# Attention stage: the score-times-value batches moved to the odd slots, with the two transposes placed directly ahead of a batch

## The chip, the core and the metric

The kernel runs on one core of a Trainium2 chip. The metric is the device time of one execution in microseconds (us). Five engines work beside each other, each through its own instruction stream in order: PE (TensorE: matrix products and transposes into PSUM banks; its weight loads are listed as PEld), DVE (VectorE), ACT (ScalarE), POOL (GpSimd) and SP (SyncE, which here only issues DMAs). They meet through semaphores: an instruction waits until a counter has reached a value.

## What is computed (the reference, cut)

```python
# x: (32 sequences, 4 channels, 250 positions); model width 64
h = tok(x, ...)                                    # 8 steps of a two-way recurrence
h = h + attn(layernorm(h), ...)                    # 8 heads of width 64
h = h + ffn(layernorm(h), ...)                     # 16 experts, the best 2 for each token

# attn, for each head:
xn = layernorm(x) * ln_scale
Q, K, V = xn @ W_q, xn @ W_k, xn @ W_v
sqdist = max(|q|^2 + |k|^2 - 2 q.k, 0)
scores = exp(-gamma * sqdist)                      # no division by a row sum
out = concat over heads of (scores @ V) @ W_o.T
```

The change touches the attention stage alone.

## The kernel before, in words

The program has three stages: the recurrence, the attention, and the mixture of experts. The 32 sequences are handled as 16 pairs, and each engine's stream is written out by hand; the order in the source is the order on the engine.

The attention stage is a software pipeline of 18 steps. In step p the engines make the projections of pair p (`new`), the scores of pair p-1 (`old`), and finish pair p-2 (`old2`). A step has eight slots, v = 0 to 7. These are the pieces, with the short names used below:

- **Token transposes** (`tokens_b`, L1064): four PE transposes that turn the normalised tokens `xn` of a pair into columns in bank 0. ACT (`round_b`, L523 and L527) and DVE (`stack_b`, L763) then make the operand `s1` of them.
- **Units u0 to u15** (`unit`, L1131 and L1135): two matmuls each, into banks 2, 3, 4 in turn. So unit k waits until unit k-3 has been read out. u0 to u7 are squared by ACT (L560), summed by POOL (L411) and DVE (L799). The four units u8, u10, u12, u14 (L1135) are read twice, first by ACT (L555, two instructions), then by DVE (L805, two instructions); u9, u11, u13, u15 are copied by ACT (L564). Slot 0 has no unit, slots 1 and 2 have three each, slots 3 to 7 two each.
- **Score products** (`scores`, L1107 and L1109): two matmuls for each of two chunks in a slot, in banks 5 to 7. ACT takes the exponential (L546), DVE clips it (`caps`, L790) in a buffer `prob`, of which there are four.
- **A batch**: the products `prob` x `u` (L1083) of two slots, 16 small matmuls in column halves, accumulated in bank 1. There are four batches for each pair. After the second and the fourth ACT copies bank 1 out (`evac_y`, L538).
- **Fold** (`fold_b`, L1091): four transposes of a finished pair into bank 0; DVE adds them to the residual (L780, L783).
- **The query and key norms**: when the eighth L799 reduction of a step is done (it stands behind u8's L805 and one clip on DVE), POOL makes `qkw` (L415, L418); PE transposes it in slot 5 (L1166), ACT and DVE make the operand `s2` of it (L584, L830), and SP carries two of its rows elsewhere by DMA.
- **The next pair's normalisation** on POOL: behind `qkw` in the same stream, ten instructions from L381 to L400, each waiting for the one before; the last, L400, writes `xn`, which the next token transposes wait for (`b_xn`).

On PE a step of the kernel before reads: token transposes; slot 0: scores, batch; slot 1: scores, u0 to u2, fold; slot 2: scores, u3 to u5, batch; slot 3: scores, u6, u7; slot 4: scores, u8, u9, batch; slot 5: scores, u10, u11, transposes of `qkw`; slot 6: scores, u12, u13, batch; slot 7: scores, u14, u15.

Of the kernel before, what the change touches and what calls it, by code (L numbers as in the profile page):

```python
# [72 lines left out]
def build(nc, cst, xin, xparts, aw1, aw2, cw1, cw2, w24, wqT, wkT, wvT, woT, wq, wk, gam, lns,  # L73
          gw, gb, w1, b1, w2, b2, fg, fb, out):
    with ExitStack() as ctx:
# [100 lines left out]
        b_xt, b_rnd, b_s1 = sem("b_xt"), sem("b_rnd"), sem("b_s1")  # L176
# [36 lines left out]
        def first_step(p):  # L213
            return p == 0
# [271 lines left out]
        def _(act):  # L486
# [53 lines left out]
            def step_b(p, j, old2, old, new, ln):  # L540
                def exps(v, c):
                    n = 2 * v + c
                    n += 16 * (p - 1)
                    act.wait_ge(b_sc, n + 1)
                    wait(act, b_pv, 8 * (p - 1) + v - 3)
                    act.activation(prob[v % PROBS][:, :, c, :], bank[5 + n % 3][0:T, 0:C].rearrange("p (h l) -> p h l", h=2),  # L546
                                   ACT.Exp).then_inc(b_exp, 1)

                def unit(k):
                    src = bank[2 + k % 3]  # L550
                    act.wait_ge(b_pj, 16 * p + k + 1)
                    if is_g(k):
                        wait(act, b_sc, 16 * (p - 1))
                        for a in range(2):
                            last = act.activation(m1[j][64 * a:64 * a + 64, k - 8 + a, :],  # L555
                                                  src[64 * a:64 * a + 64, 0:C], ACT.Copy)
                        last.then_inc(b_ev, 1)
                    elif k < 8:
                        wait(act, b_sum, 8 * p + k - 1)
                        act.activation(sq[k % 2][:, :, :], src[0:T, :].rearrange("p (h d) -> p h d", h=H), ACT.Square)\  # L560
                            .then_inc(b_ev, 1)
                    else:
                        wait(act, b_pv, 8 * (p - 1))
                        act.activation(u_sb[j][:, (k - 8) // 2, :], src[0:T, :], ACT.Copy).then_inc(b_ev, 1)  # L564

                for v in range(8):
                    if new and v == 0 and not first_step(p):
                        round_b(p, j)
                    rest = list(units(v)) if new else []
                    for c in range(2):  # L570
                        if old:
                            exps(v, c)
                        if rest:
                            unit(rest.pop(0))
                    if v == 0 and old2:
                        evac_y(p - 2, 1)
                    if v == 4 and old:
                        evac_y(p - 1, 0)
                    for k in rest:
                        unit(k)  # L580
                    if new and v == 5:
                        act.wait_ge(b_qt, p + 1)
                        wait(act, b_s2, p)
                        act.activation(rnd2[64:S_ROWS, :], bank[0][64:S_ROWS, 0:C], ACT.Copy).then_inc(b_rnd2, 1)  # L584
                    if p == PAIRS:
                        start_c(v)
# [80 lines left out]
        def _(dve):  # L667
# [117 lines left out]
            def step_b(p, j, old2, old, new, ln):  # L785
# [27 lines left out]
                for v in range(8):  # L813
                    if new and v == 0 and not first_step(p):
                        stack_b(p, j)
                    rest = list(units(v)) if new else []
                    for c in range(2):
                        if old2 and v == 3 and c == 0:
                            residual(p - 2, 1)
                        if rest:  # L820
                            unit(rest.pop(0))
                        if old:
                            caps(v, c)
                    for k in rest:
                        unit(k)
                    if v == 2 and old2:
                        residual(p - 2, 0)
                    if new and v == 5:
                        dve.wait_ge(b_rnd2, p + 1)
                        dve.scalar_tensor_tensor(s2[j][64:S_ROWS, :], f32(rnd2[64:S_ROWS, :]),  # L830
                                                 c_sb[64:S_ROWS, C_MS2:C_MS2 + 1], bank[0][64:S_ROWS, 0:C],
                                                 ALU.mult, ALU.add).then_inc(b_s2, 1)
                    if ln and v == 0:
                        norm_stats(p + 1, b_ln)
                    if ln and v == 1:
                        norm_aggr(p + 1, b_ln)
                    if p == PAIRS:
                        start_c(v)
# [143 lines left out]
        def _(pe):  # L982
# [77 lines left out]
            def tokens_b(p):  # L1060
                pe.wait_ge(b_xn, p + 1)
                wait(pe, b_s2, p)
                for c in range(CH):
                    last = pe.transpose(bank[0][:, c * T:(c + 1) * T],  # L1064
                                        xn[:, c, :, :].rearrange("p a d -> p (a d)"), ident[0:T, 0:T])
                last.then_inc(b_xt, 1)
# [28 lines left out]
            def step_b(p, j, old2, old, new, ln):  # L1095
# [41 lines left out]
                    last.then_inc(b_pj, 1)  # L1137

                for v in range(8):
                    if new and v == 0 and not first_step(p):  # L1140
                        tokens_b(p)
                    if old and v == 0:
                        pe.wait_ge(b_row, 32 * p)
                    rest = list(units(v)) if new else []
                    for c in range(2):
                        if old:
                            scores(v, c)
                        if rest:
                            unit(rest.pop(0))
                    for k in rest:  # L1150
                        unit(k)
                    for n in (v - 2, v - 1) if v % 2 == 0 else ():
                        for hh in range(2):
                            if v == 0 and old2:
                                products(p - 2, n + 8, j, hh)
                            if v > 0 and old:
                                products(p - 1, n, o, hh)
                    if old2 and v == 1:
                        if new:
                            pe.wait_ge(b_s1, p + 1)  # L1160
                        fold_b(p - 2)
                    if new and v == 5:
                        pe.wait_ge(b_qkw, 2 * p + 2)
                        wait(pe, b_res, p - 1)
                        for c in range(CH):
                            last = pe.transpose(bank[0][0:S_ROWS, c * T:(c + 1) * T], qkw[:, c, :], ident[0:T, 0:T])  # L1166
                        last.then_inc(b_qt, 1)
                    if p == PAIRS:
                        start_c(v)
# [191 lines left out]
```

## Time and profile before

| | |
|---|---|
| median of 3 runs | 797.2 us (796.36 to 800.66) |
| the profiled execution | 796.95 us, of which the span from first to last instruction is 795.1 us |
| granted TensorE clock, mean | 0.981 of full speed |
| busy share of the span | PE 95%, DVE 78%, ACT 67%, POOL 59% |
| attention stage, whole steps | from 139.6 us to 462.9 us, 13 steps of 24.87 us |

A step is read from one pair's token transposes to the next pair's. The times in the rows are microseconds from the start of the span.

### The profile page before, as it was taken

Reading aid. Unit: us, or ns where it says so; the run is one execution under the profiler, and the core shown is the slowest. Engines: PE = TensorE matmul, PEld = TensorE weight load, DVE = VectorE, ACT = ScalarE, POOL = GpSimd, SP = SyncE. Lnnn points to the kernel's source line nnn. Section 1 sums busy time; section 2 is a strip of 40 time slices with the busy share of each in tenths; the row PEclk is TensorE's granted clock in tenths of the full one; section 3 lists DMA queues with packets and bytes.
Section 4 is the critical chain, followed back from the end, with each engine's and each line's share of the span. In section 5 each row is a group of like instructions: output and inputs, shape, how many; then the busy total and the mean of one; then the engine's idle time right before and its main releaser. Section 6 shows DMA issues by size and latency. Waiting matters only on the chain.

```text
span 795.1 us, 16732 instructions
## 1 busy us (share of the span) xinstructions
PE 751.7 (95%) x5680; PEld 435.9 (55%) x5680; DVE 620.8 (78%) x1524; ACT 534.4 (67%) x1058; POOL 468.6 (59%) x628
## 2 busy tenths in 40 slices
PE   2999879999999999999999998999999999999992
PEld 1343456666666666766667665535445455454441
DVE  3677657888878888788887886688888888888862
ACT  0566578888888888888888888554554555545442
POOL 8650256455464554645556452257888788887877
PEclk9999969999999999999999999899999999999997
DMA  6400021112211122111221112000000000000000
GB/s 151 137 2 2 1 54 29 40 41 54 54 29 40 42 54 54 28 40 41 55 54 28 40 42 54 1 2 2 9 8 15 9 8 9 9 15 8 8 8 19
DMA packets 22859, 25.69 MB, mean 32 GB/s; under 512 B 12888, under 2 KB 21720, under 8 KB 22648
## 3 DMA queue, kind: packets, MB, share of 16 engines
q1 hardware_dynamic: 21608, 23.57, 12.8%
q10 hardware_dynamic: 1168, 1.07, 0.6%
q8 instruction: 46, 0.75, 0.4%
q14 instruction: 37, 0.30, 0.1%
HBM read 5.30 MB, written 2.43 MB: 10 GB/s over the span
## 4 chain that ended last, share of the span: by engine, by line
PE 72%; DVE 11%; ACT 6%; issue 6%; POOL 3%; DMA 1%; SPq 0%; POOLq 0%; ACTq 0%; DVEq 0%
PE bank L1220 14%; PE bank L1198 13%; PE bank L1083 10%; PE bank L1131 9%; PE bank L1011 6%; PE bank L1107 6%; DVE m L805 5%; PE bank L1109 5%; DVE prob L790 4%; ACT m L555 3%; PE bank L1001 2%; ACT prob L546 1%; PE bank L1245 1%; PE bank L1237 1%; PE bank L1253 1%
## 5 line engine op out<-in xcount | busy, mean ns | idle before, releaser
L790 DVE TENSOR_SCALAR prob<-prob,cap_hi,cap_lo 125x500 f32<-125x500 f32 x256 | 155.8, 636 | 45.5 <-ACT prob L546 43.4
L411 POOL TENSOR_TENSOR sq<-sq 125x256 f32<-125x256 f32 x128 | 97.9, 776 | 151.1 <-ACT sq L560 127.3
L546 ACT ACTIVATE prob<-bank 125x500 f32<-125x500 f32 x256 | 148.9, 592 | 40.8 <-PE bank L1109 38.8
L1198 PE MATMUL bank<-cs,w_sb 64*64 64x500 f32 x1024 | 147.3, 580 | 2.5 <-DVE gated L921 2.4
L1220 PE MATMUL bank<-gated,w_sb 64*64 64x500 f32 x1024 | 149.1, 588 | 0.0
L448 POOL TENSOR_TENSOR gated<-relu,wb 128x500 f32<-128x500 f32 x96 | 120.2, 1253 | 48.3 <-ACT relu L645 45.8
L921 DVE SCALAR_TENSOR_TENSOR gated<-bank,nb,wb 128x500 f32<-128x500 f32 x160 | 114.9, 727 | 34.5 <-PE bank L1198 34.5
L1083 PE MATMUL bank<-prob,u 125*64 125x250 f32 x1024 | 127.4, 386 | 1.9
L645 ACT ACTIVATE relu<-bank,b_sb 128x500 f32<-128x500 f32 x96 | 64.7, 674 | 92.6 <-PE bank L1198 92.6
L1107 PE MATMUL bank<-m,s 128*125 128x500 f32 x256 | 111.5, 435 | 0.2 <-DMA m<-s 0.2
L805 DVE TENSOR_TENSOR m<-bank,m 64x500 fp32r<-64x500 f32 x128 | 86.5, 676 | 27.5 <-ACT m L555 26.2
L1109 PE MATMUL bank<-m,s 112*125 112x500 f32 x256 | 101.2, 395 | 0.0
L1083 PEld LDWEIGHTS bank<-prob,u 125*64 125x64 f32 x1024 | 65.4, 137 | 58.9 <-DVE prob L790 24.7
L1131 PE MATMUL bank<-wqku_hi,s 128*125 128x512 f32 x192 | 79.7, 415 | 5.8 <-DVE s L763 3.0
L1198 PEld LDWEIGHTS bank<-cs,w_sb 64*64 64x64 f32 x1024 | 52.9, 133 | 55.4 <-issue 48.8
L560 ACT ACTIVATE sq<-bank 125x512 f32<-125x512 f32 x128 | 75.6, 600 | 7.7 <-PE bank L1131 3.7
L1131 PE MATMUL bank<-wqku_lo,s 128*125 128x512 f32 x192 | 77.5, 404 | 0.0
L555 ACT ACTIVATE m<-bank 64x500 fp32r<-64x500 f32 x128 | 74.0, 578 | 1.0 <-PE bank L1135 0.2
L1220 PEld LDWEIGHTS bank<-gated,w_sb 64*64 64x64 f32 x1024 | 46.8, 132 | 45.4 <-issue 38.6
L1107 PEld LDWEIGHTS bank<-m,s 128*125 128x125 f32 x256 | 48.3, 189 | 30.4 <-issue 17.8
L1011 PE MATMUL bank<-st_a,w_sb 64*64 64x500 f32 x224 | 58.2, 591 | 0.0
L1011 PE MATMUL bank<-st_b,w_sb 64*64 64x500 f32 x224 | 57.4, 591 | 0.0
(171 smaller groups left out, 1319.1 us busy)
## 6 DMA issues: line engine op xcount, KB each, us to landing
m<-m SPq DMA_DIRECT2D x128, 125.0 KB, 2.3
out<-res SPq DMA_DIRECT2D x16, 125.0 KB
xa<-xparts SPq DMA_DIRECT2D x4, 281.2 KB
w_sb<-in_w SPq DMA_DIRECT2D x1, 1024.0 KB
xw<-xparts SPq DMA_DIRECT2D x4, 140.6 KB
w_sb<-in_w SPq DMA_DIRECT2D x1, 512.0 KB
m<-s SPq DMA_DIRECT2D x32, 15.6 KB
xparts<-x_part SPq DMA_DIRECT2D x1, 375.0 KB, 4.5
```

Of the source, the lines that this page charges most:

```text
L448: gp.tensor_tensor(gated[g % 8][:, :], relu_sb[n % 3][:, :], wb[q % 2][:, :], ALU.mult).then_inc(c_gatep, 1)
L546: act.activation(prob[v % PROBS][:, :, c, :], bank[5 + n % 3][0:T, 0:C].rearrange("p (h l) -> p h l", h=2), ACT.Exp).then_inc(b_exp, 1)
L790: dve.tensor_scalar(part, part, cap_hi[0:T, h:h + 1], cap_lo[0:T, h:h + 1], ALU.min, ALU.max)\
L805: last = dve.tensor_tensor(m2[j][0:64, h, :], bank[2 + k % 3][rows, 0:C], f32(m1[j][rows, h, :]), ALU.subtract)
L921: dve.scalar_tensor_tensor(gated[g % 8][:, :], up_bank(g)[:, 0:C], nb1[:, g:g + 1], wb[q % 2][:, :], ALU.max, ALU.mult).then_inc(c_gated, 1)
L1011: last = pe.matmul(dst[cols, 0:C].rearrange("p (b l) -> p b l", b=2), w24_sb[rows, 0, :], src[rows, :, 0:L], start=False, stop=True)
L1083: last = pe.matmul(bank[1][64 * c:64 * c + 64, 0:L], u_sb[jj][:, 2 * b + c, h * D:(h + 1) * D], prob[v % PROBS][:, hh, c, :], start=h == 0 ...
L1107: pe.matmul(ps, s1[o][:, cols], m1[o][:, 2 * hp:2 * hp + 2, b * L:(b + 1) * L], start=True, stop=False)
L1109: pe.matmul(ps, s2[o][:, cols], m2[o][:, 2 * hp:2 * hp + 2, b * L:(b + 1) * L], start=False, stop=True).then_inc(b_sc, 1)
L1131: last = pe.matmul(dst[0:T, :], s1[j][:, c * T:(c + 1) * T], w[:, q, :], start=first, stop=not first)
L1198: last = pe.matmul(up_bank(g)[cols, 0:C], w1_sb[rows, g, cols], cs1[q % 3][rows, :], start=True, stop=True)
L1220: last = pe.matmul(y[cols, 0:C], w2_sb[rows, g, :], gated[g % 8][rows, :], start=v == 0, stop=v == 7, skip_group_check=True)
```

## The change

On PE the batches move from the even slots to the odd ones, each of them one slot later. The fold moves from slot 1 to slot 3, directly ahead of the batch there, and the explicit wait for `b_s1` ahead of it goes (u0 waits for that semaphore too). The token transposes of the next pair move from the head of the next step to the end of slot 7, behind u15 as now, but ahead of the batch of that slot. On ACT the two `evac_y` move two slots later; on DVE the two residual instructions move two slots later.

```diff
@@ ACT, step_b @@
-                    if v == 0 and old2:
+                    if v == 2 and old2:
                         evac_y(p - 2, 1)
-                    if v == 4 and old:
+                    if v == 6 and old:
                         evac_y(p - 1, 0)
@@ DVE, step_b @@
-                        if old2 and v == 3 and c == 0:
+                        if old2 and v == 5 and c == 0:
                             residual(p - 2, 1)
...
-                    if v == 2 and old2:
+                    if v == 4 and old2:
                         residual(p - 2, 0)
@@ PE, step_b @@
                 for v in range(8):
-                    if new and v == 0 and not first_step(p):
-                        tokens_b(p)
...
-                    for n in (v - 2, v - 1) if v % 2 == 0 else ():
+                    if old2 and v == 3:
+                        fold_b(p - 2)
+                    if ln and v == 7:
+                        tokens_b(p + 1)
+                    for n in (v - 3, v - 2) if v % 2 else ():
                         for hh in range(2):
-                            if v == 0 and old2:
+                            if v == 1 and old2:
                                 products(p - 2, n + 8, j, hh)
-                            if v > 0 and old:
+                            if v > 1 and old:
                                 products(p - 1, n, o, hh)
-                    if old2 and v == 1:
-                        if new:
-                            pe.wait_ge(b_s1, p + 1)
-                        fold_b(p - 2)
```

On PE, around the end of a step: the last unit u15 (into bank 2), the token transposes (into bank 0), and what follows them, in the kernel before. L1107 and L1109 are the score products, L1083 the batch.

```order
L1131 MATMUL bank2<-wqku_hi,s1_0 125x512
L1131 MATMUL bank2<-wqku_lo,s1_0 125x512
L1064 MATMUL bank0<-c_sb,xn 128x125 x4
L1107 MATMUL bank7<-m1_0,s1_0 125x500
L1109 MATMUL bank7<-m2_0,s2_0 125x500
L1107 MATMUL bank5<-m1_0,s1_0 125x500
L1109 MATMUL bank5<-m2_0,s2_0 125x500
L1083 MATMUL bank1<-prob2,u1 64x250 x4
L1083 MATMUL bank1<-prob3,u1 64x250 x4
```

The same place in the changed kernel:

```order
L1131 MATMUL bank2<-wqku_hi,s1_0 125x512
L1131 MATMUL bank2<-wqku_lo,s1_0 125x512
L1064 MATMUL bank0<-c_sb,xn 128x125 x4
L1083 MATMUL bank1<-prob0,u1 64x250 x4
L1083 MATMUL bank1<-prob1,u1 64x250 x4
L1107 MATMUL bank7<-m1_0,s1_0 125x500
L1109 MATMUL bank7<-m2_0,s2_0 125x500
L1107 MATMUL bank5<-m1_0,s1_0 125x500
L1109 MATMUL bank5<-m2_0,s2_0 125x500
```

The batch behind the token transposes is the one (of `prob0` and `prob1`) that stood in slot 6 before, ahead of u14 and u15; the one of `prob2` and `prob3` now follows in slot 1.

On PE, from u9 (into bank 2) to u11 (into bank 4) in slots 4 and 5 of the kernel before; u8, just ahead, went into bank 4 too, and the L1135 rows are u10 (into bank 3).

```order
L1131 MATMUL bank2<-wqku_hi,s1_0 125x512
L1131 MATMUL bank2<-wqku_lo,s1_0 125x512
L1083 MATMUL bank1<-prob2,u1 64x250 x4
L1083 MATMUL bank1<-prob3,u1 64x250 x4
L1107 MATMUL bank7<-m1_1,s1_1 125x500
L1109 MATMUL bank7<-m2_1,s2_1 125x500
L1135 MATMUL bank3<-s1_0,wg_hi 128x500
L1135 MATMUL bank3<-s1_0,wg_lo 128x500
L1107 MATMUL bank5<-m1_1,s1_1 125x500
L1109 MATMUL bank5<-m2_1,s2_1 125x500
L1131 MATMUL bank4<-wqku_hi,s1_0 125x512
L1131 MATMUL bank4<-wqku_lo,s1_0 125x512
```

The same place in the changed kernel:

```order
L1131 MATMUL bank2<-wqku_hi,s1_0 125x512
L1131 MATMUL bank2<-wqku_lo,s1_0 125x512
L1107 MATMUL bank7<-m1_1,s1_1 125x500
L1109 MATMUL bank7<-m2_1,s2_1 125x500
L1135 MATMUL bank3<-s1_0,wg_hi 128x500
L1135 MATMUL bank3<-s1_0,wg_lo 128x500
L1107 MATMUL bank5<-m1_1,s1_1 125x500
L1109 MATMUL bank5<-m2_1,s2_1 125x500
L1131 MATMUL bank4<-wqku_hi,s1_0 125x512
L1131 MATMUL bank4<-wqku_lo,s1_0 125x512
L1083 MATMUL bank1<-prob2,u1 64x250 x4
L1083 MATMUL bank1<-prob3,u1 64x250 x4
```

No batch stands between u8 and u11 any more; it comes behind u11. In the same way the batch between u12 and u15 has gone behind u15.

On DVE, slot 4 and the start of slot 5 in the changed kernel: the read of u8 (L805 from bank 4), the clips, the eighth reduction (L799), and the two residual instructions (L780, L783).

```order
L805 TENSOR_TENSOR m2_1<-bank4,m1_1 64x500 x2
L790 TENSOR_SCALAR prob0<-prob0,cap_hi,cap_lo 125x500
L799 TENSOR_REDUCE qk<-sq2_1 125x8
L790 TENSOR_SCALAR prob0<-prob0,cap_hi,cap_lo 125x500
L780 TENSOR_TENSOR z2<-bank0,h_all 125x256
L783 TENSOR_TENSOR h_all<-bank0,z2 125x256
L805 TENSOR_TENSOR m2_1<-bank3,m1_1 64x500 x2
L790 TENSOR_SCALAR prob1<-prob1,cap_hi,cap_lo 125x500 x2
```

In the kernel before the rows are the same without L780 and L783, which stood in slots 2 and 3: the eighth reduction keeps its place behind u8's L805 and one clip.

## Rows read from the trace of the kernel before

**Rows 1.** The page, part 1: busy time and share of each engine.

```profile
PE 751.7 (95%) x5680; PEld 435.9 (55%) x5680; DVE 620.8 (78%) x1524; ACT 534.4 (67%) x1058; POOL 468.6 (59%) x628
```

**Rows 2.** The waits: who waited for whom, us in total, times, longest.

```profile
PEld bank L1083 <- DVE prob L790: 24.7, 66, 0.6
...
PEld bank L1064 <- POOL xn L400: 6.1, 15, 1.6
```

**Rows 3.** Timeline of PE in one step: start, duration, engine, line, operands.

```profile
263.88 0.65 PE L1064 MATMUL bank<-c_sb,xn 125*128 125x125 f32 x4
...
265.38 2.29 PE L1083 MATMUL bank<-prob,u 125*64 125x250 f32 x16
...
277.10 0.39 PE L1135 MATMUL bank<-s,wg_hi 128*128 128x500 f32 x1
...
278.24 0.39 PE L1131 MATMUL bank<-wqku_lo,s 128*125 128x512 f32 x1
278.56 1.91 PE L1083 MATMUL bank<-prob,u 125*64 125x250 f32 x16
280.40 0.49 PE L1107 MATMUL bank<-m,s 128*125 128x500 f32 x1
280.73 0.39 PE L1109 MATMUL bank<-m,s 112*125 112x500 f32 x1
280.95 0.40 PE L1135 MATMUL bank<-s,wg_hi 128*128 128x500 f32 x1
...
284.25 0.50 PE L1131 MATMUL bank<-wqku_hi,s 128*125 128x512 f32 x1
284.59 0.39 PE L1131 MATMUL bank<-wqku_lo,s 128*125 128x512 f32 x1
...
288.74 0.65 PE L1064 MATMUL bank<-c_sb,xn 125*128 125x125 f32 x4
```

**Rows 4.** Timeline of PE: token transposes of the third and of the last pair.

```profile
139.57 0.65 PE L1064 MATMUL bank<-c_sb,xn 125*128 125x125 f32 x4
...
462.88 0.65 PE L1064 MATMUL bank<-c_sb,xn 125*128 125x125 f32 x4
```

**Rows 5.** Timeline of DVE in the same step as Rows 3.

```profile
274.70 0.41 DVE L780 TENSOR_TENSOR z<-bank,h_all 125x256 f32<-125x256 f32 x1
...
280.91 0.41 DVE L799 TENSOR_REDUCE qk<-sq 125x8 f32<-125x256 f32 x1
...
284.23 0.99 DVE L790 TENSOR_SCALAR prob<-prob,cap_hi,cap_lo 125x500 f32<-125x500 f32 x2
...
287.61 1.80 DVE L790 TENSOR_SCALAR prob<-prob,cap_hi,cap_lo 125x500 f32<-125x500 f32 x2
```

**Rows 6.** Timeline of POOL in the same step; in brackets the idle time before.

```profile
281.40 0.55 POOL L415 TENSOR_TENSOR qkw<-qk,gneg 125x64 f32<-125x64 f32 x1 [2.41 <-DVE qk L799]
...
282.47 1.02 POOL L383 TENSOR_TENSOR inv<-inv,mhalf 125x4 f32<-125x4 f32 x1
...
284.41 1.23 POOL L391 TENSOR_TENSOR inv<-inv,mhalf 125x4 f32<-125x4 f32 x1
...
287.39 1.29 POOL L400 TENSOR_TENSOR xn<-z,lns_sb 125x512 f32<-125x512 f32 x1
```

**Rows 7.** Timeline of PE where the attention stage ends.

```profile
489.88 2.12 PE L1083 MATMUL bank<-prob,u 125*64 125x250 f32 x16
494.10 0.62 PE L1237 MATMUL bank<-c_sb,cxn 125*128 125x125 f32 x4 [2.10 <-ACT cxn L613]
```

**Rows 8.** Windows of PE: stretch, length, busy (instructions), granted clock, DMA share, GB/s.

```profile
493.00:494.00 1.00, 0.00 (x0) 1.00 0.00 0
...
496.00:497.00 1.00, 1.00 (x15) 0.50 0.00 0
...
501.00:502.00 1.00, 1.00 (x8) 0.50 0.00 0
```

**Rows 9.** Groups by line: count, busy us, mean ns, idle us before.

```profile
L538 ACT ACTIVATE y_att<-bank 128x250 f32<-128x250 f32 x32 | 12.2, 382 | 15.6 <-PE bank L1083 15.6
```

## The prediction

> **What bounds the kernel now.** The page's first part comes first: PE is busy 95% of the span, the other engines 78% and less [rows 1]. By that alone PE is the bound, and every wait taken from PE is time won. The list of waits says which there are: PE's weight loads stood 24.7 us before clips (66 times, about one for each of the 64 batches), and 6.1 us, 15 times, before POOL's `xn` [rows 2]. The first sum looks like the prize. The timeline of PE in one step corrects that: a batch in slot 4 begins 0.32 us after the last matmul of a unit (278.24 to 278.56) and takes 1.91 us, the one in slot 0 takes 2.29 us [rows 3]. So of the time before clips only 0.38 us for each step is lost on PE, in slot 0; the rest is a fixed step into the batch's other shape.
>
> The second sum is the smaller one, and it is the one that matters. The last of POOL's ten instructions ends at 287.39 + 1.29 = 288.68 [rows 6], and PE's token transposes begin at 288.74 [rows 3], 0.06 us later. They don't begin when PE has come to them; they begin when `xn` is there. It is a wait that hardly shows, because PE comes there at about the same moment. Followed back: POOL's stretch begins at 281.40 with L415, which stood idle 2.41 us until DVE's L799 [rows 6]; that reduction ends at 280.91 + 0.41 = 281.32 [rows 5], 4.22 us after u8 began on PE at 277.10 [rows 3]. So there are two paths from u8 to the next token transposes, each of 11.64 us (277.10 to 288.74): PE's own work, and the path u8 - ACT - DVE - L799 (4.22) - POOL (288.68 - 281.32 = 7.36) - `xn`. From the transposes on to the next u8 there is PE's own work alone: 277.10 - 263.88 = 13.22 [rows 3]. Together 24.86, and the 13 whole steps (462.88 - 139.57)/13 give 24.87 [rows 4].
>
> **The change part by part.** The sum is made for a step, as time from token transposes to u8, and from u8 to token transposes.
>
> *What a batch costs PE.* From the last unit matmul before it to the second score matmul behind it 280.73 - 278.24 = 2.49 us; without the batch two matmul starts of 0.23 each (five of them from 277.10 to 278.24 make 1.14). So 2.03.
>
> *From the transposes to u8.* Now two batches lie there (slots 0 and 2). In the changed order there are three: one directly behind the transposes, one in slot 1, one in slot 3 behind the fold. That adds 2.03. The clip wait of slot 0 goes: -0.38. The step into a batch partly coincides with the transposes, and u8 now stands behind a batch, so that ACT and DVE are free for it: I take 0.15 off for both, an estimate between 0 and 0.3. The sum is 13.22 + 2.03 - 0.38 - 0.15 = 14.7.
>
> *From u8 to the transposes, on PE.* Two batches become one: 11.64 - 2.03 = 9.6. But a batch has covered something there. u13 waits for the bank of u10 (u10 at 280.95, u13 at 284.25, its second matmul 0.34 later) [rows 3]: 3.30 us is what ACT and DVE need for such a unit, and PE now loses about 0.11 before u13 and 0.11 behind, 0.22. In the changed order this pair is covered by a batch (-0.22), while u8 to u11 and u12 to u15 stand without one: six pairs of matmuls of 0.46 are 2.75, so PE waits 3.30 - 2.75 = 0.55, and 0.11 behind, twice: +1.3. PE would be there after 9.6 - 0.2 + 1.3 = 10.7.
>
> *From u8 to the transposes, by POOL.* Nothing in that path is shortened. The eighth reduction stands on DVE behind u8's L805 and one clip, as before (the residual instructions come behind it), and POOL's ten follow. 11.6 us remain. PE, there after 10.7, waits some 0.9, and the batch in slot 7 that could be done meanwhile stands behind the waiting transposes in PE's stream. Everything else on PE waits with it; ACT and DVE have caught up by then, and wait for PE.
>
> So a step is 14.7 + 11.6 = 26.3 to 26.4 instead of 24.87: +1.5. Bounds: 1.3 (0.3 off, as above) and 1.65 (nothing off), and the same whatever u11 and u15 lose, as long as that stays under the 0.9.
>
> *POOL's stretch beside other work.* Its instructions are longer beside clips: L391 took 1.23 where its like L383 took 1.02 [rows 6], while two clips that take 0.99 together took 1.80 beside L400 [rows 5]. In the changed order other clips fall beside POOL's last three. I take nothing for it and keep +-0.2 a step. The Trainium skill has a harder rule (SBUF — State Buffer, Who interferes with whom): of a VectorE and a GpSimd instruction that need the shared port pair, the later one is blocked until the first has ended. If a clip came just ahead of L400, that would add up to one clip, half of 0.99, to each step, +6 us in all; L400 at 1.29 beside the clips of 1.80 agrees with the rule, with POOL first.
>
> *Parts that I cost at nothing.* `evac_y` (0.38 each [rows 9]) in slot 6 must be done before the batch of slot 7 may write bank 1: that batch now waits for `xn` anyway, over 1 us longer than ACT needs. The residual pair on DVE (0.41 each [rows 5]) lies ahead of u10's L805, whose bank u13 needs only after a batch; uncovered it would cost 0.8. The removed wait for `b_s1` is made by u0. The `qkw` transposes come behind the batch of slot 5, and ACT waits at L584 for them with the exponentials of slot 6 queued behind; PE has three score banks and the unit banks ahead, so it doesn't run dry; if it did, u15 would be later, inside the 0.9. SP's DMAs keep their order and are issued earlier relative to their use.
>
> *First and last steps.* Up to the third pair's transposes (139.57) nothing is lost: step 1 has the same batches on both sides. Then 13 steps x 1.5 = 19.5. After the last token transposes the changed order has one batch more to do than now (2.03), without the losses of slot 0 and u13 (-0.38 - 0.22), with those of u11 and u15 (2 x 0.66): +2.7. The first transposes of the expert stage stand idle 2.10 for ACT's normalisation [rows 7]; that wait stays, since in the changed order the exponentials stand ahead of it as now.
>
> Sum: 796.95 (the profiled execution: 795.1 of span and 1.85 around it) + 19.5 + 2.7 = 819.2; the median of the runs shown, 797.2, is 0.25 above the profiled one. I predict 819.
>
> **Rivals.**
>
> *POOL's path gives way.* If `xn` came earlier than I think, PE would set the step: 14.7 + 10.7 = 25.4, +0.55 x 13 + 2.7 = +10, 807. Against it: all ten instructions and what they wait for are unchanged.
>
> *PE alone counts (faster).* PE's share of 95% speaks for it. Then only losses are removed, 0.38 in slot 0, 0.22 at u13, and some 0.05 at the transposes: -0.65 x 14 = -9, 788. It decides if L400 ends over 1.5 us earlier relative to u8 and u11 doesn't wait; against it the 0.06 us in rows 3 and 6, and the 3.30 between u10 and u13.
>
> *The waits only change places (same).* If the won 0.6 and the lost 1.3 met with a POOL path that is shorter by just that, the step would stay at 24.9: 797 to 800.
>
> *The clock falls.* In the changed order PE would stand idle three times in each step, about 0.5, 0.5 and 0.7 us. After an idle of 2.10 [rows 7] the granted clock fell from 1.00 (2.4 GHz) to 0.50 (1.2 GHz), and six windows in a row, 496 to 502, read 0.50 [rows 8]. If each step lost as much, six such microseconds at half speed would cost 3 a step, 13 x 3 = 39 more: 858. Against it: the idle times are shorter by far and not in one piece. The Trainium skill speaks for it (TensorE: Matmul & The Clock Gate, A second HAM failure mode: psum-queue depth-cycling): frequent short idles between groups of matmuls, as banks are cycled, can make the clock swing between its levels. By that rule the time would be this rival's 858; no row here shows it for idles under 1 us.
>
> **How the numbers follow.** The forecast: 0.78, by itself 814 to 825. POOL's path gives way: 0.07. PE alone: 0.06. Waits change places: 0.04. Clock: 0.05. The range of 8 in 10 takes in the forecast and the first rival, 806 to 826, with POOL's +-0.2 a step (2.6). A measurement can tell 0.5% (4 us) from no change: faster 0.06, same 0.04, slower 0.90.
>
> **What would show it.** Right: token transposes 26.2 to 26.5 apart, beginning 0.05 to 0.06 after L400's end, PE idle ahead of them, L400 still 7.4 after the eighth reduction; u11 and u15 waiting for L805, u13 not; batches all of 1.91, none with 2.29. Wrong: steps of 25.4 or less, or transposes that begin well after `xn` is there, or windows of the steady steps with a clock of 0.50, or waits of POOL that are shorter from the reduction to `xn`.

## The result and the profile after

The changed kernel takes 830.0 us (median of 4 runs, 826.9 to 837.3); the kernel before, run beside it, 797.4. The ratio is 1.0415, with a 95% interval of 1.0341 to 1.0489: slower. The prediction said 819 with a range of 806 to 826. The direction and the mechanism held, the size didn't, and the time lies outside the range.

The profiled execution of the changed kernel took 826.9 us, with a span of 825.1. The page's first part answers to [rows 1]; the columns are the same.

```profile
PE 755.5 (92%) x5680; PEld 443.3 (54%) x5680; DVE 618.4 (75%) x1524; ACT 526.8 (64%) x1058; POOL 472.8 (57%) x628
```

Every engine does the same number of instructions as before, and TensorE is busy 3.8 us longer in a span that is 30.0 us longer. So 26 of the 30 us are idle time of TensorE. The list of waits answers to [rows 2].

```profile
PEld bank L1131 <- DVE m L805: 31.1, 32, 2.3
PEld bank L1064 <- POOL xn L400: 21.3, 15, 2.0
...
PE bank L1064 <- POOL xn L400: 14.8, 15, 1.6
...
PEld bank L1083 <- DVE prob L790: 7.5, 22, 0.5
```

The waits for clips, which looked like the prize, fell from 24.7 to 7.5 us. The wait for `xn`, which looked small, is now in TensorE's own list: 14.8 us, 15 times. And the value units u11 and u15 wait for L805, 32 times.

The timeline of TensorE in one step answers to [rows 3].

```profile
193.97 0.65 PE L1064 MATMUL bank<-c_sb,xn 125*128 125x125 f32 x4 [0.98 <-POOL xn L400]
194.54 1.91 PE L1083 MATMUL bank<-prob,u 125*64 125x250 f32 x16
...
208.90 0.39 PE L1135 MATMUL bank<-s,wg_hi 128*128 128x500 f32 x1
...
212.19 0.50 PE L1131 MATMUL bank<-wqku_hi,s 128*125 128x512 f32 x1 [0.40 <-DVE m L805]
...
216.55 0.40 PE L1131 MATMUL bank<-wqku_hi,s 128*125 128x512 f32 x1
...
219.08 0.50 PE L1131 MATMUL bank<-wqku_hi,s 128*125 128x512 f32 x1 [0.54 <-DVE m L805]
219.41 0.39 PE L1131 MATMUL bank<-wqku_lo,s 128*125 128x512 f32 x1
220.78 0.65 PE L1064 MATMUL bank<-c_sb,xn 125*128 125x125 f32 x4 [0.97 <-POOL xn L400]
```

From token transposes to u8 it is 208.90 - 193.97 = 14.93, from u8 to the next token transposes 220.78 - 208.90 = 11.88, together 26.81 where before it was 24.86. u11 and u15 wait, u13 (216.55) doesn't; the batch takes 1.91; TensorE stands idle 0.97 before the transposes. GpSimd's and VectorE's timelines of the same step answer to [rows 5, 6].

```profile
213.12 0.55 POOL L415 TENSOR_TENSOR qkw<-qk,gneg 125x64 f32<-125x64 f32 x1 [4.00 <-DVE qk L799]
...
215.85 0.46 POOL L389 TENSOR_TENSOR inv<-inv,eps 125x4 f32<-125x4 f32 x1
216.39 1.18 POOL L391 TENSOR_TENSOR inv<-inv,mhalf 125x4 f32<-125x4 f32 x1
...
219.31 1.41 POOL L400 TENSOR_TENSOR xn<-z,lns_sb 125x512 f32<-125x512 f32 x1
```

```profile
212.63 0.41 DVE L799 TENSOR_REDUCE qk<-sq 125x8 f32<-125x256 f32 x1
...
219.06 1.94 DVE L790 TENSOR_SCALAR prob<-prob,cap_hi,cap_lo 125x500 f32<-125x500 f32 x2
```

L400 ends at 219.31 + 1.41 = 220.72, 0.06 before the transposes: GpSimd's path binds, in each of the 13 whole steps. The reduction ends at 213.04, 4.14 after u8 began (before 4.22). From there to the end of L400 it is 7.68 us, where before it was 7.36. Two instructions make the difference: L400 takes 1.41 for 1.29 [rows 6], and L389 takes 0.46 (L391 is 0.05 shorter); the kernel before has

```profile
284.13 0.20 POOL L389 TENSOR_TENSOR inv<-inv,eps 125x4 f32<-125x4 f32 x1
```

Three of the 13 steps are longer still, 28.4 us. In these TensorE's clock fell, which it did in no whole step of the kernel before. First TensorE's timeline, then its windows of one microsecond (stretch, length, busy, granted clock, DMA share, GB/s), which answer to [rows 8].

```profile
246.19 0.40 PE L1131 MATMUL bank<-wqku_lo,s 128*125 128x512 f32 x1
247.56 0.99 PE L1064 MATMUL bank<-c_sb,xn 125*128 125x125 f32 x4 [0.97 <-POOL xn L400]
248.47 3.19 PE L1083 MATMUL bank<-prob,u 125*64 125x250 f32 x16
```

```profile
247.00:248.00 1.00, 0.44 (x3) 0.86 0.93 202
248.00:249.00 1.00, 1.00 (x7) 0.50 0.68 150
...
250.00:251.00 1.00, 1.00 (x6) 0.50 0.00 0
```

The batch behind the transposes took 3.19 instead of 1.91 us, and such a step lost 1.63 us. The same happens at 357 and 466 us. Now the account closes: 13 steps of +1.92 make 25.0, three falls of 1.63 make 4.9, the steps up to the third pair's transposes cost 0.7 (they begin at 140.26, before at 139.57), and after the last transposes the changed kernel needs 331.5 us, 0.7 less than before. 25.0 + 4.9 + 0.7 - 0.7 = 29.9, and the spans differ by 30.0.

### The profile page after: what moved, and what is told of

It is laid out like the page before. It is cut to its first block, busy times and chain, and to the rows that moved or that the text cites. A ratio compares the mean times of both kernels' runs of the same rounds, so it can differ in the third digit from the quotient of the medians.

```text
span 825.1 us, 16718 instructions
## 1 busy us (share of the span) xinstructions
PE 755.5 (92%) x5680; PEld 443.3 (54%) x5680; DVE 618.4 (75%) x1524; ACT 526.8 (64%) x1058; POOL 472.8 (57%) x628
## 4 chain that ended last, share of the span: by engine, by line
PE 71%; POOL 13%; DVE 7%; ACT 3%; issue 3%; ACTq 1%; DMA 1%; POOLq 0%; DVEq 0%
PE bank L1218 14%; PE bank L1196 13%; PE bank L1083 12%; PE bank L1131 7%; PE bank L1011 6%; PE bank L1107 5%; PE bank L1109 4%; DVE m L805 3%; POOL xn L400 2%; ACT m L555 2%; POOL inv L391 2%; POOL inv L383 2%; PE bank L1001 2%; PE bank L1064 1%; DVE prob L790 1%
## 5 line engine op out<-in xcount | busy, mean ns | idle before, releaser
L790 DVE TENSOR_SCALAR prob<-prob,cap_hi,cap_lo 125x500 f32<-125x500 f32 x256 | 152.2, 622 | 65.5 <-ACT prob L546 63.4
L1083 PE MATMUL bank<-prob,u 125*64 125x250 f32 x1024 | 126.4, 390 | 0.1
L805 DVE TENSOR_TENSOR m<-bank,m 64x500 fp32r<-64x500 f32 x128 | 86.3, 674 | 34.5 <-ACT m L555 33.1
L1107 PE MATMUL bank<-m,s 128*125 128x500 f32 x256 | 107.6, 420 | 0.0
L1109 PE MATMUL bank<-m,s 112*125 112x500 f32 x256 | 101.1, 395 | 0.0
L1131 PE MATMUL bank<-wqku_hi,s 128*125 128x512 f32 x192 | 81.4, 424 | 20.4 <-DVE m L805 17.5
L1083 PEld LDWEIGHTS bank<-prob,u 125*64 125x64 f32 x1024 | 69.8, 140 | 44.6 <-issue 10.7
L1107 PEld LDWEIGHTS bank<-m,s 128*125 128x125 f32 x256 | 48.2, 188 | 27.2 <-issue 17.9
L1131 PEld LDWEIGHTS bank<-wqku_hi,s 128*125 128x125 f32 x192 | 36.7, 191 | 42.8 <-DVE m L805 31.1
```

Source lines behind the costliest of these rows:

```text
L790: dve.tensor_scalar(part, part, cap_hi[0:T, h:h + 1], cap_lo[0:T, h:h + 1], ALU.min, ALU.max)\
L805: last = dve.tensor_tensor(m2[j][0:64, h, :], bank[2 + k % 3][rows, 0:C], f32(m1[j][rows, h, :]), ALU.subtract)
L1083: last = pe.matmul(bank[1][64 * c:64 * c + 64, 0:L], u_sb[jj][:, 2 * b + c, h * D:(h + 1) * D], prob[v % PROBS][:, hh, c, :], start=h == 0 ...
L1107: pe.matmul(ps, s1[o][:, cols], m1[o][:, 2 * hp:2 * hp + 2, b * L:(b + 1) * L], start=True, stop=False)
L1109: pe.matmul(ps, s2[o][:, cols], m2[o][:, 2 * hp:2 * hp + 2, b * L:(b + 1) * L], start=False, stop=True).then_inc(b_sc, 1)
L1131: last = pe.matmul(dst[0:T, :], s1[j][:, c * T:(c + 1) * T], w[:, q, :], start=first, stop=not first)
```

## The experiments

Ten kernels were run. "Step" is the time from one pair's token transposes to the next pair's. The table gives the median time of the runs, and from each trace the usual step among those where the clock did not fall, its two parts, and by how much the transposes begin after `xn` is ready. The row of e6 comes from an execution whose clock was lower throughout (see there).

| kernel | us | step | to u8 | from u8 | after `xn` |
|---|---|---|---|---|---|
| before | 797.4 | 24.87 | 13.22 | 11.64 | 0.05 |
| changed | 830.0 | 26.79, three 28.4 | 14.91 | 11.88 | 0.05 |
| e1 transposes behind the batch | 818.9 | 26.52 | 13.83 | 12.69 | 0.84 |
| e2 scales early | 811.7 | 26.05 | 14.83 | 11.22 | 3.52 |
| e3 batch (4,5) alone | 832.2 | 26.53, five 28.13 | 14.90 | 11.63 | 0.06 |
| e4 filler | 824.0 | 26.82 | 14.91 | 11.91 | 0.06 |
| e5 short clips | 807.6 | 25.72 | 14.89 | 10.83 | 0.06 |
| e6 batch (6,7) alone | 832.4 | 26.87, four 28.4 | 15.0 | 11.88 | 0.61 |
| e7 the same, scales early | 825.1 | 26.65 | 14.85 | 11.81 | 3.65 |
| e8 before, scales early | 807.8 | 25.62 | 13.01 | 12.61 | 3.55 |
| e9 before, scales spread | 795.2 | 24.79 | 13.18 | 11.60 | 3.83 |
| e10 the same, `xn` held | 794.1 | 24.62 | 13.02 | 11.60 | 1.25 |

**e1: the token transposes behind the batch of slot 7.** Of the changed kernel, so that TensorE doesn't stand with a batch queued behind its wait.

```diff
-                    if ln and v == 7:
-                        tokens_b(p + 1)
                     for n in (v - 3, v - 2) if v % 2 else ():
                         ...
+                    if ln and v == 7:
+                        tokens_b(p + 1)
```

> The changed kernel with one part undone: the token transposes stand behind the batch of slot 7 again, just ahead of the next step's scores. Theory (PE stands idle before the transposes because xn comes 11.9 us after u8, and the batch of slot 7 is queued behind them): that batch now fills the wait, so u8 to transposes is set by PE, 10.8 + 2.0 = 12.8, with no idle of a microsecond ahead of the transposes and no window of the steady steps at a clock of 0.50. Behind the transposes the cover for u0 is gone: u0 waits some 0.7 us for s1, so transposes to u8 is 14.9 - 2.05 + 0.7 = 13.6. Step 26.3 to 26.4, time 797 + 13 x 1.5 = 816. Rival (the loss is that u8 to u11 and u12 to u15 stand without a batch; where the transposes stand is no matter): as the changed kernel, 827 to 830, step 26.8.

Measured: 818.9 us, ratio 1.0261 (1.0232 to 1.0290). The step is 26.52, 0.1 above what was expected, no whole step shows a clock below 1.00, and the wait for `xn` is gone. In its place TensorE waits for the next pair's operand `s1`:

```profile
272.49 0.65 PE L1064 MATMUL bank<-c_sb,xn 125*128 125x125 f32 x4
...
275.26 0.46 PE L1131 MATMUL bank<-wqku_hi,s 128*125 128x512 f32 x1 [0.73 <-DVE s L763]
```

The batch in slot 7 had covered the way from the transposes through ScalarE and VectorE to u0, and without it u0 waits.

**e2: GpSimd's seven scale instructions ahead of its wait for the eighth reduction.** Of the changed kernel. They don't need that reduction, and only stood behind it in GpSimd's stream.

```diff
+                    if ln:
+                        b_scales(p + 1)          # L381 to L393 of before
                     gp.wait_ge(b_red, 8 * p + 8)
                     ...
                 if ln:
-                    b_scales(p + 1)
+                    b_tokens(p + 1)              # the last three, to xn
```

> The changed kernel, PE, ACT and DVE untouched; on POOL the seven small instructions of the next pair's normalisation (L381 to L393) stand ahead of the wait for the eighth reduction, where POOL is idle for 3.95 us. Theory: xn is there 3 to 4 us earlier relative to u8, the wait before the transposes goes, PE sets the stretch from u8 to the transposes at 10.8 and the step at 14.9 + 10.8 = 25.7; no clock of 0.50 in the steady steps; time 797 + 13 x 0.85 = 808, the rest of the loss being the two waits of u11 and u15 (0.65 and 0.75). Rival (POOL's path is not what PE waits for, the batches' missing cover is): 827 to 830, step 26.8.

Measured: 811.7 us, ratio 1.017 (1.0141 to 1.0199); the step is 26.05, 0.35 more than expected. GpSimd's path is out of the way and 18 us of the 33 came back: by the two profiled executions 15.3, of which the 13 shorter steps make 9.6 and the clock falls that did not come 4.9. TensorE's own order keeps the rest: behind u8 it is 11.22 instead of 11.64, though a batch of 2.03 has left that side, since u11 waits 0.40 and u15 0.95 there. The 0.35 stand at u15 (lines are 5 higher than before in this kernel): TensorE's timeline and VectorE's.

```profile
293.39 0.50 PE L1136 MATMUL bank<-wqku_hi,s 128*125 128x512 f32 x1 [0.95 <-DVE m L810]
293.73 0.39 PE L1136 MATMUL bank<-wqku_lo,s 128*125 128x512 f32 x1
293.96 0.59 PE L1069 MATMUL bank<-c_sb,xn 125*128 125x125 f32 x4
```

```profile
289.56 1.61 DVE L795 TENSOR_SCALAR prob<-prob,cap_hi,cap_lo 125x500 f32<-125x500 f32 x2
291.20 0.74 DVE L835 SCALAR_TENSOR_TENSOR s<-rnd,c_sb,bank 48x500 fp32r<-48x500 f32 x1
291.97 1.36 DVE L810 TENSOR_TENSOR m<-bank,m 64x500 fp32r<-64x500 f32 x2
```

The last GpSimd instruction (1.30 us from 289.14 on) now runs beside two clips, which take 1.61 instead of 0.99; the rounding residual behind them comes 0.6 later, measured from u8, the L805 behind that 0.5 later, and u15 waits 0.95 instead of 0.54.

**e3: one batch alone.** The kernel before, with only the batch (4,5) moved from slot 6 to behind the next token transposes in slot 7.

```diff
-                    for n in (v - 2, v - 1) if v % 2 == 0 else ():
+                    if ln and v == 7:
+                        tokens_b(p + 1)
+                    for n in {0: (-2, -1), 2: (0, 1), 4: (2, 3), 7: (4, 5)}.get(v, ()):
```

> The kernel before with one part of the change alone: only the batch of slot 6 moves, to the end of slot 7 behind the token transposes; the other three batches, the fold, evac_y and the residual stay in their old slots, and u8 to u11 keeps its batch. Theory (two paths of 11.6 to 11.9 from u8 to the transposes; work taken from PE's path ahead of them only makes PE wait, and it has to be done behind them): the step grows by the whole batch, 14.85 + 11.7 = 26.5, less or more 0.2; 797 + 13 x 1.7 = 819, up to 824 if the clock falls in some steps. Rival (the loss is the missing cover of u11 and u15): only u15 loses 0.75 and slot 0 wins its 0.38, 24.87 + 0.4 = 25.3, 802.

Measured: 832.2 us, ratio 1.0414 (1.0368 to 1.0461). The step is the theory's, and the time lies above it by the clock: it fell in five of the 13 steps (1.6 each) and twice more behind the last transposes, from where this kernel needs 4.8 us more than the one before. One batch of four, moved past the token transposes, makes 1.66 of the changed kernel's 1.92 a step: from u8 to the transposes it is still 11.63, since GpSimd sets that, and the other part has the batch on top. TensorE now idles where the batch had been:

```profile
273.25 0.50 PE L1131 MATMUL bank<-wqku_hi,s 128*125 128x512 f32 x1 [1.30 <-DVE m L805]
274.33 0.95 PE L1064 MATMUL bank<-c_sb,xn 125*128 125x125 f32 x4 [0.35 <-POOL xn L400]
```

**e4: the idle time filled.** The changed kernel with four matmuls, read by nobody, in the wait for `xn`.

```diff
+                    if ln and old and v == 7:
+                        wait(pe, b_s2, p + 1)
+                        for _ in range(FILL):                # FILL = 4
+                            pe.matmul(bank[0][0:T, :], s1[j][:, 0:T], wqku_hi[:, 0, :], start=True, stop=True)
                     if ln and v == 7:
                         tokens_b(p + 1)
```

> The changed kernel with four matmuls that nobody reads (0.23 us each) on PE between u15 and the token transposes of every step, in the time when PE waits for xn. Theory (POOL sets the step, and three of the 13 steps are 1.6 us longer because the clock falls after the idle ahead of the transposes): the step stays at 26.8, L1064 still begins 0.05 after L400 ends, and no window of the steady steps reads a clock of 0.50; 827 - 3 x 1.6 = 822, and the executions agree with each other. Rival 1 (the clock falls for another reason): 827 to 830, with windows of 0.50. Rival 2 (PE is the bound): the step grows by 0.9, 827 + 12 = 839.

Measured: 824.0 us, ratio 1.0323 (1.029 to 1.0356). More work on TensorE, and a faster kernel: its four runs (822.4 to 825.4) lie below all four of the changed one. All 13 steps take 26.80 to 26.84, and in none of them does the clock fall below 1.00; the end of one wait:

```profile
301.11 0.40 PE L1131 MATMUL bank<-wqku_lo,s 128*125 128x512 f32 x1
301.34 1.08 PE L1155 MATMUL bank<-wqku_hi,s 128*125 128x512 f32 x4
302.49 0.65 PE L1064 MATMUL bank<-c_sb,xn 125*128 125x125 f32 x4
```

So in the changed kernel the falls hang on the idle time ahead of the transposes, and they are a loss of their own on top of it. Without them the changed order takes 824.0 us.

**e5: short clips.** The changed kernel, in which the clips work on 16 columns instead of 500 (most of the clipping is left out).

```diff
-                    part = prob[v % PROBS][:, hh, :, :]
+                    part = prob[v % PROBS][:, hh, :, 0:8]
```

> The changed kernel with VectorE's clips cut from 500 to 16 columns (most of the clipping is left out; VectorE's instruction count and every wait stay). Theory: GpSimd's ten instructions from the eighth reduction to the normalized tokens take 7.69 us in the changed kernel because VectorE's clips run beside them (the last one, 1.42 us, beside a clip that takes 1.49 instead of 0.54); the same chain without clips beside it, at the second pair, took 6.88. So the chain falls to 6.9 to 7.1 and the last instruction to 1.27 to 1.30; reductions and residuals come earlier too, and the step falls from 26.79 to 25.4 to 26.1, about 808 to 815 us. Rival: the added 0.31 us of the chain comes from something else than the clips (the residual of the rounded scales, ScalarE, or the place in the step): the chain stays at 7.5 or above and the step above 26.4, at 818 us or more.

Measured: 807.6 us (one run), step 25.72. GpSimd's stretch from the eighth reduction to `xn` takes 6.88 us instead of 7.68, at every step. Three of its instructions:

```profile
288.45 0.20 POOL L389 TENSOR_TENSOR inv<-inv,eps 125x4 f32<-125x4 f32 x1
288.73 1.01 POOL L391 TENSOR_TENSOR inv<-inv,mhalf 125x4 f32<-125x4 f32 x1
...
291.49 1.27 POOL L400 TENSOR_TENSOR xn<-z,lns_sb 125x512 f32<-125x512 f32 x1
```

0.20, 1.01 and 1.27 where the changed kernel has 0.46, 1.18 and 1.41, and the one before 0.20, 1.23 and 1.29. So it is VectorE's clips that lengthen GpSimd's path, by 0.8 us in the changed kernel and by 0.5 in the one before.

**e6: the batch (6,7) alone, to slot 1.** Since e3 had shown that batches are needed in slots 4 and 6, this one left them there and moved the one that waited 0.38 us for clips in slot 0.

```diff
-                    for n in (v - 2, v - 1) if v % 2 == 0 else ():
+                    for n in {1: (-2, -1), 2: (0, 1), 4: (2, 3), 6: (4, 5)}.get(v, ()):
```

> The kernel before with only the batch of products (6,7) moved, from slot 0 to slot 1; fold, evacuation and residuals follow it as in the change (slots 3, 2, 4 and 5); the batches of slots 2, 4 and 6 and the token transposes stay. Theory: batches at slots 4 and 6 are what covers the waits for the value units' banks, and they stay; the batch that waited 0.38 us for clipped probabilities at slot 0 no longer does, so the step falls from 24.87 to about 24.49 and the time to 792 (790 to 794.5). Rival: any batch that is taken out of slot 0 leaves the path through GpSimd as long as it was and the residuals in slots 4 and 5 lengthen it (VectorE's queue): step 24.9 to 25.3, 798 to 803 us.

Measured: 832.4 us, ratio 1.0451 (1.0413 to 1.0488). My theory fell, and the rival that I had set beside it was not the cause either: the transposes begin 0.61 us after `xn`, so GpSimd's path does not bind. The mean clock of five of its runs was 0.97, which is part of it, but the step itself shows the main thing:

```profile
279.45 0.60 PE L1064 MATMUL bank<-c_sb,xn 125*128 125x125 f32 x4
...
283.25 0.47 PE L1131 MATMUL bank<-wqku_hi,s 128*125 128x512 f32 x1 [1.81 <-DVE s L763]
```

The batch in slot 0 covered a wait as well, that of u0 for `s1`. It paid 0.38 us for clips, and hid 1.8. I had e1's row with the same wait before me, and didn't draw on it. The profiled execution was the longest of the six (840.9 us, mean clock 0.927), and its windows read 0.95 where those of the other kernels read 1.00:

```profile
277.00:278.00 1.00, 1.00 (x8) 0.95 0.06 10
```

So its figures are not to be compared to the hundredth. e7, at 1.00, has the same wait.

**e7 and e8: the scales early, in e6 and in the kernel before.** The edit is that of e2.

> The same with GpSimd's scale instructions ahead of its wait for the eighth reduction, so that the token transposes never wait for GpSimd. Theory: TensorE bounds the step in it and in the kernel before as well (transposes 0.27 us after the matmul ahead of them), so the early scales take away 0.05 us a step at most: 24.44 to 24.5, 791 to 792 us. Rival: the path through GpSimd bounds the step there too, and its release gives 0.3 us a step or more: 24.2 or below, 788 us or less. Second rival: the last GpSimd instruction now falls beside a clip ahead of VectorE's rounding residual and delays the last value unit, as in the run with early scales of the changed kernel (0.46 us a step): 24.9, 797 us.

> The kernel before with GpSimd's scale instructions ahead of its wait for the eighth reduction and nothing else. Theory: no change, since TensorE bounds the step of the kernel before and the path through GpSimd ends just ahead of it: step 24.8 to 24.87, 796 to 798 us. Rival: the delayed clip costs 0.3 to 0.5 us a step, 801 to 804 us.

Measured: e7 825.1 us, ratio 1.0338 (1.031 to 1.0367); e8 807.8, ratio 1.0118 (1.0092 to 1.0145). e7 rests on e6's mistake: u0 still waits, here with the clock at 1.00.

```profile
276.82 0.47 PE L1136 MATMUL bank<-wqku_hi,s 128*125 128x512 f32 x1 [1.29 <-DVE s L768]
```

e8 is slower than the kernel before, and by another cause than my rival's. From its list of waits:

```profile
PE bank L1171 <- POOL qkw L423: 15.7, 15, 1.6
```

The seven scale instructions now stand ahead of `qkw` in GpSimd's stream and make it late; TensorE's transposes of `qkw` wait 1.0 us in each step. In e2 they stand behind a batch and hardly wait.

**e9 and e10: the scales in GpSimd's idle times.** The kernel before, with two scale instructions behind the fourth halved sum, three behind the sixth and two behind the eighth (e9), and with L400 held until VectorE has written the rounding residual L830 (e10).

```diff
+                        if ln and k in (3, 5, 7):
+                            b_scales(p + 1, k // 2 - 1)      # two, three, two of the seven
...
+                wait(gp, b_s2, p)                             # e10 alone, ahead of xn
```

> The kernel before with GpSimd's seven scale instructions spread over its idle times between the halved sums (two behind the fourth sum, three behind the sixth, two behind the eighth), so that neither its products for the qkw transposes nor VectorE's reductions come later, and nothing else. Theory: in the run with the scales ahead of the wait, 1.2 us a step went to the qkw transposes, which GpSimd served late; here they wait no longer, the batch in slot 0 no longer waits 0.38 us for a clip that ran beside GpSimd's last instruction, and TensorE alone bounds the step: 24.5 to 24.7 for 24.87, 792 to 795.5 us. Rival 1: the last GpSimd instruction now stretches a clip in slot 5, VectorE's rounding residual and the last value unit come late, and the step is 24.9 to 25.3, 798 to 803 us. Rival 2: no change within 0.3%, since the token transposes, no longer preloaded ahead of a wait, take as much as the stall gives back.

> The kernel before with the spread scales, and GpSimd's last instruction of the chain (the normalized tokens) held until VectorE has written the residual of the rounded scales. Theory: in the run with spread scales that instruction ran beside a clip (0.91 instead of 0.54 us) and moved the rounding residual and with it SyncE's row DMA 0.34 us later, for which the first scores behind the token transposes waited 0.35 us; held back, it runs beside VectorE's subtractions from PSUM, which keep their 0.67 to 0.68 us, and no clip is longer than 0.6; the scores start 0.4 us behind the transposes and the step is 24.4 to 24.55, 790 to 792.5 us. Rival: a subtraction or another instruction of VectorE is stretched in the clip's place, or the DMA wait has another cause, and the step stays at 24.7 to 24.9, 794 to 797 us.

Measured: e9 795.2 us, ratio 0.9958 (0.9942 to 0.9975); e10 794.1, ratio 0.9945 (0.9925 to 0.9966). Both are about half a percent faster than the kernel before, and their intervals overlap, so e10 is not shown to be faster than e9 by the times; the step shows it. e9's step fell by 0.08 only: two clips beside `xn` take 1.36 us, the rounding residual and the row DMA behind it come later, and the first score products wait for that DMA (weight loads of TensorE).

```profile
264.24 0.18 PEld L1116 LDWEIGHTS bank<-m,s 128*125 128x125 f32 x1 [0.35 <-DMA m<-s]
```

In e10 that is gone. GpSimd's `xn` runs beside VectorE's subtractions, one of whose two inputs lies in PSUM, and neither is stretched:

```profile
283.84 1.28 POOL L406 TENSOR_TENSOR xn<-z,lns_sb 125x512 f32<-125x512 f32 x1 [2.67 <-DVE s L840]
```

```profile
283.89 1.36 DVE L815 TENSOR_TENSOR m<-bank,m 64x500 fp32r<-64x500 f32 x2 [0.22 <-ACT m L565]
285.29 0.99 DVE L800 TENSOR_SCALAR prob<-prob,cap_hi,cap_lo 125x500 f32<-125x500 f32 x2
```

The Trainium skill says the same (SBUF — State Buffer, Who interferes with whom): a VectorE instruction with at most one input in SBUF, outside the modes that use two ports, doesn't contend with GpSimd. The step is 24.62, 0.07 above the upper end of what I expected, since the batch in slot 0 still waits for a clip (it takes 2.14 us instead of 1.91); the median is 1.6 us above it.

## Why the prediction was right, and where it was wrong

- **GpSimd's path binds: right.** Transposes begin 0.05 to 0.06 us after `xn` in every step of the changed kernel [rows 3, 6], and e2, which takes that path away, has steps that are 0.74 shorter. That TensorE alone would need 10.7 from u8 to the transposes was right too: e5, where it waits less than 0.1 there, has 10.83.
- **A third batch between the transposes and u8: right, 0.2 short.** The traces give 14.91. 13.22 + 2.03 - 0.38 is 14.87; the 0.15 that I took off for batch steps that coincide was not there. e3 has the same 14.9 with one batch moved, so it is the number of batches on that side that counts.
- **The step that failed, first term: "I take nothing for it", GpSimd's stretch beside other work.** Together with "11.6 us remain" and the 0.15 it made the term +1.5 a step. Measured: from u8 to the transposes 11.88 instead of 11.64 (GpSimd 0.31 longer, the reduction 0.07 earlier), and with the 0.2 above +1.92. e5 shows the cause: without long clips the stretch is 6.88. The bound of 0.2 a step that I kept for it was too small for 0.31. Of 13 steps this makes 25.0 instead of 19.5. By itself it would have left the time inside the range.
- **The step that failed, second term: the clock, which the sum has at nothing and a rival at 39 us, with a chance of 0.05.** It came in part: windows of 0.50 in the steady steps, which the prediction itself named as a sign of being wrong. I priced it as a loss in every step and set it against idle times under 1 us. It came in 3 of 13 steps of the profiled execution and cost 4.9 us. e4 shows that it hangs on the idle time before the transposes, which I had foreseen, with 0.7 to 0.9 us a step, and that it is what carries the time out of the range: with that wait filled and steps of the same length the median is 824.0. The other timed runs of the changed kernel have lower mean clocks (0.976, 0.975 and 0.937, against 0.981) and are longer, 829.7 to 837.3; whether by more falls or, as in e6's profiled execution, by a lower clock throughout, no trace shows. The rule that I cited (the Trainium skill, TensorE: Matmul & The Clock Gate, A second HAM failure mode: psum-queue depth-cycling) speaks of swings between the two levels behind frequent short idles, and the trace agrees with it in kind: from 1.00 to 0.50 and back, three times in 13 steps, behind idle times of 0.55 and 0.97 us.
- **The end: +2.7 forecast, -0.7 measured.** What I left out was that the kernel before loses its clock there, from 495.6 to 502.4 us [rows 8], and the changed one doesn't. By an estimate half of these 6.8 us, 3.4, is lost, and 2.7 - 3.4 = -0.7. e4 bears the half out: it has the changed kernel's order there, a clock of 0.50 from 522.0 to 525.4, and needs 333.2 us instead of 331.5, 1.7 more. So the terms of the 2.7 fit, and a loss of the kernel before hid them.
- **All of it.** The forecast for the profiled execution was 819.2, and it took 826.9: 5.5 more in the steps, 4.9 by the falls, 0.7 up to the third pair's transposes and 3.4 less at the end make the 7.7. That the falls and the end cancel in part is luck.
- **Parts costed at nothing: right.** In the 13 whole steps TensorE's waits are those for `xn` and for L805; none for `evac_y`, the residual pair or `b_s1` is among them.

What stays open is why the clock falls in some steps and not in others of the same length, and how often it does from run to run. Nor is the wait before the transposes the only one behind which it falls: e6's transposes wait for nothing, u0 waits 1.81 us in one piece, and the clock fell in four steps; e7 waits 0.30 and 1.29 in the same place, and it fell in none.

## What to carry to other kernels

A busy engine's small wait (0.05 us before the transposes) can be two paths that end together; find the second path before work is moved from one side of that point to the other, since what leaves one side comes back as idle time and what arrives on the other side is paid in full. Ask of every large block what the instruction behind it would wait for without it: in this kernel the batches of slots 0, 4 and 6 each hid a wait of 0.4 to 1.8 us, and the 0.38 us that one of them lost in the open was its price. And a path that runs through GpSimd is as long as VectorE's work beside it makes it: the same twelve instructions, from `qkw` to `xn`, took 6.88, 7.36 or 7.68 us, by the clips beside them.

## What the hardware showed that was not expected

- The clock fell behind idle times that are short. In the changed kernel it fell to 0.50 in three steps, in each of which TensorE had stood idle 0.55 us before u15 and 0.97 us before the transposes; ten steps with the same idle times kept 1.00. Where the attention stage ends, TensorE idled 2.31 us in one piece, and the clock stayed:

```profile
525.31 0.62 PE L1235 MATMUL bank<-c_sb,cxn 125*128 125x125 f32 x4 [2.31 <-ACT cxn L613]
```

```profile
526.00:527.00 1.00, 1.00 (x6) 1.00 0.00 0
```

  The kernel before, idle 2.10 us at the same place [rows 7], fell to 0.50 behind it [rows 8]. So the length of one idle time alone doesn't decide it.
- VectorE's clips and GpSimd stretch each other, and not evenly. Beside L400 two clips of 0.99 took 1.94 in the changed kernel (219.06 to 221.00), and L400 1.41 instead of 1.27: most of the delay falls on the clip. The second clip ended 0.28 after L400 (220.72). So did the clip beside L400 in the kernel before (287.61 + 1.35 = 288.96, L400's end 288.68), and in every whole step of every kernel but e5 and e10 the clip that was running when that instruction ended was done 0.27 to 0.28 later, whether it had begun 0.12 (e8) or 0.66 us (e9) after L400 did. A clip of 500 columns alone takes 0.54 and one of 16 columns (e5) 0.29, so that by an estimate 0.25 of a clip goes with its columns, about what was left to do when L400 ended; a short clip of e5, which has hardly any such work, was done 0.03 after it. The Trainium skill (the section on SBUF cited above) has the later of two such instructions blocked until the first ends. The trace agrees: by these numbers only the clip's fixed part, some 0.3, ran beside L400.
